# Attention kernel on one core: one product with ones per group of heads, the first pair of key tiles added on VectorE

## The reference

```
h   = layernorm(x) * (scale + 1) + shift
q,k,v = split(h @ w_qkv)                      # 16 heads of 32 channels
q,k = rope(layernorm(q, q_norm_w)), rope(layernorm(k, k_norm_w))
attn = softmax(q @ k^T / sqrt(32))            # 512 x 512 for each head
out = x + (attn @ v) @ w_out * gate
```

## Time and profile before

| | |
|---|---|
| three timed runs | 1797.75 us median (1791.26 to 1800.73) |
| the profiled execution | 1788.8 us, of which 1787.0 us is the span from the first to the last instruction |
| PE busy | 1679.0 us, 94% of the span |
| DVE, ACT, POOL busy | 1245.0, 1036.3, 644.8 us |
| DMA queue of POOL (q0) | 133.18 MB, 39.0% of 16 engines' span |
| granted TensorE clock | 0.980 of full speed, mean over the span |

### The profile page before, as it was taken

One profiled execution on the slowest core, in us unless ns is written; L12 is line 12 of the kernel. 1 busy time (PEld: TensorE's weight loads), 2 busy tenths in 40 slices (PEclk: granted clock), 3 DMA queues, 4 the chain that ended last, 5 costly groups with the idle time before them and its releaser, 6 DMA issues.

```text
span 1787.0 us, 32167 instructions
## 1 busy us (share of the span) xinstructions
PE 1679.0 (94%) x12334; PEld 985.3 (55%) x12334; DVE 1245.0 (70%) x1603; ACT 1036.3 (58%) x1547; POOL 644.8 (36%) x709
## 2 busy tenths in 40 slices
PE   5968999999999999999999999999999999998777
PEld 2734555555555555555555555555555555555444
DVE  8667667777777767777776777777677777766543
ACT  2436556666666666666666666666666665665552
POOL 2423243334334334433433443343344334334222
PEclk8979999999999999999999999999999999999998
DMA  6015355555546555554555555555555555545454
GB/s 208 25 39 109 77 132 112 117 126 111 123 110 137 113 115 127 113 121 110 135 114 116 128 113 118 113 133 115 113 130 113 118 113 133 116 95 118 104 110 124
DMA packets 55566, 205.38 MB, mean 115 GB/s; under 512 B 6888, under 2 KB 6888, under 8 KB 39160
## 3 DMA queue, kind: packets, MB, share of 16 engines
q0 software_dynamic: 18288, 133.18, 39.0%
q1 hardware_dynamic: 37128, 70.14, 11.6%
HBM read 53.25 MB, written 16.88 MB: 39 GB/s over the span
## 4 chain that ended last, share of the span: by engine, by line
PE 85%; ACT 7%; DVE 4%; issue 2%; DMA 1%; SPq 0%; DVEq 0%; ACTq 0%; POOLq 0%
PE SA L412 13%; PE Y L326 11%; PE Y L339 10%; PE Y L329 9%; PE Y L333 9%; PE MB L440 7%; ACT probs L746 7%; PE SM L382 7%; PE O L431 7%; PE MB L361 3%; PE SA L416 3%; DVE cst L987 2%; PE SA L316 1%; PE SA L390 1%; DMA probs<-in_L_cond_w_qkv_dram 1%
## 5 line engine op out<-in xcount | busy, mean ns | idle before, releaser
L987 DVE TENSOR_REDUCE cst<-SM 128x2 fp32r<-128x1024 f32 x256 | 313.4, 1224 | 342.8 <-PE MB L382 342.8
L1208 POOL DMA_DIRECT2D probs<-probs x127 | 109.8, 865 | 812.6 <-ACT probs L748 794.0
L746 ACT ACTIVATE probs<-SM 128x1024 f32<-128x1024 f32 x256 | 262.2, 1024 | 234.8 <-PE SM L416 227.4
L987 DVE TENSOR_REDUCE cst<-MB 128x2 fp32r<-128x1024 f32 x256 | 311.1, 1215 | 0.0
L431 PE MATMUL O<-probs,vals 128*32 128x512 f32 x2048 | 273.8, 607 | 0.0
L748 ACT ACTIVATE probs<-SA 128x1024 f32<-128x1024 f32 x256 | 260.9, 1019 | 0.0
L646 ACT ACTIVATE rows<-Y 128x512 f32<-128x512 f32 x121 | 72.4, 598 | 267.1 <-PE Y L333 267.1
L326 PE MATMUL Y<-wqkv_hi,hT_hi 128*128 128x512 f32 x716 | 216.0, 424 | 0.0
L382 PEld LDWEIGHTS SM<-qk_hi 32*128 32x128 f32 x512 | 51.3, 183 | 258.9 <-issue 78.6
L329 PE MATMUL Y<-wqkv_hi,hT_lo 128*128 128x512 f32 x716 | 193.2, 391 | 0.4 <-DVE hT_lo L969 0.4
L333 PE MATMUL Y<-wqkv_lo,hT_hi 128*128 128x512 f32 x716 | 191.6, 389 | 0.0
(11 more groups left out here) (199 smaller groups left out, 3473.9 us busy)
## 6 DMA issues: line engine op xcount, KB each, us to landing
probs<-probs POOLq DMA_DIRECT2D x127, 1024.0 KB, 7.7
xin<-in_x_dram SPq DMA_DIRECT2D x62, 256.0 KB, 6.8
xres<-in_x_dram SPq DMA_DIRECT2D x60, 256.0 KB, 2.6
out_dram<-xres SPq DMA_DIRECT2D x60, 256.0 KB, 3.7
shift_scale<-mod_rows SPq DMA_DIRECT2D x15, 512.0 KB, 6.0
gate<-mod_rows SPq DMA_DIRECT2D x16, 256.0 KB, 5.2
rows<-in_L_cond_mod_w_dram SPq DMA_DIRECT2D x2, 1024.0 KB, 8.8
probs<-in_L_cond_w_qkv_dram SPq DMA_DIRECT2D x2, 1024.0 KB, 13.2
```

The costliest lines, as they stand in the source:

```text
L746: act.activation(probs[:, a, 2:4, :], SM[:], ACT.Exp).then_inc(s_exp, 1)
L987: dve.tensor_reduce(heads[:, 2 * half:2 * half + 2, 0], bank[:], AX.X, ALU.max, negate=True).then_inc(max_out, 1)
L1208: pool.dma_start(probs[:, probs_buffer(t - 1)].rearrange("p h n -> p (h n)"), probs[:, probs_buffer(t)].rearrange("p h n -> p (h n)"), acc ...
```

## The change

Five things change together, in every stage.

1. The pair is added on DVE. A new function `add_pair(s)` waits for `first_added` and for `weigh_values(s, 2)`, and adds buffer 0 to buffer 2 in one instruction over 128 x 2048 elements. It stands on DVE behind the fourth `maxima` of the stage. The second accumulating transfer, `add_keys(s, 3)`, now waits for this addition (`pair_added`) in place of `weigh_values`. So buffer 2 ends with the sum of all four key tiles.
2. There is one product with ones per group in place of two: `add_over_keys(s - 1)` stands behind `project_out` and before `scores_by_key(s, 2)` of the next stage. The products behind `scores_by_key(s, 1)` and `scores_by_key(s, 3)` are gone.
3. `move_first_sum` on ACT and `add_sums` on DVE are gone. `log_sums` reads PSUM directly and stands, with `inverse_sums`, later on ACT, behind `x_high` and `guess_roots`. `scores_by_query(g, 2)` waits for `sum_ln`; the waits of `scores_by_query(g, 1)` and `(g, 3)` for the sums are gone. The exponentials of tile 0 wait for `pair_added`.
4. On DVE `square_sums(s + 5, 0)` moves from before `low_qk` to behind `maxima(s + 1, 0)`, and `normalize_x` moves from behind the fourth `maxima` to before it.
5. On POOL `add_residual` moves behind the two rotations. At the end of the kernel two products with ones take the place of three, and `add_pair` of the last group stands before `last_parts` on DVE.

```diff
--- before.py
+++ after.py
@@ -131,7 +132,6 @@
             sem("h_hi"), sem("squared"), sem("raw_out"), sem("v_out"), sem("o_out"), sem("qk_high"))
         cT_out, s_exp, sum_ln, sum_ready = sem("cT_out"), sem("s_exp"), sem("sum_ln"), sem("sum_ready")
-        first_summed = sem("first_summed")
         root_ln, root_guess = sem("root_ln"), sem("root_guess")
@@ -142,7 +142,7 @@
         x_scaled, h_lo, qk_low, max_out, o_scaled, y_gated = (
             sem("x_scaled"), sem("h_lo"), sem("qk_low"), sem("max_out"), sem("o_scaled"), sem("y_gated"))
-        sum_added, pass_set = sem("sum_added"), sem("pass_set")
+        pair_added, pass_set = sem("pair_added"), sem("pass_set")
         o_high, o_low, last_high, last_low, wout_low = (
@@ -368,10 +368,8 @@
                     if g == 0:
                         pe.wait_ge(mod_out, 4)
-                if t == 1 and g >= 2:
-                    pe.wait_ge(sum_added, g - 1)
-                if t == 3 and g >= 1:
-                    pe.wait_ge(first_summed, g)
+                if t == 2 and g >= 2:
+                    pe.wait_ge(sum_ln, g - 1)
                 if n > 0:
@@ -433,18 +431,18 @@
                 mm.then_inc(pv_step, 1)
 
-            def add_over_keys(g, t, bank):
-
-                pe.wait_ge(first_added if t == 0 else second_added, 16 * (g + 1))
+            def add_over_keys(g, bank):
+
+                pe.wait_ge(second_added, 16 * (g + 1))
                 for i in range(HG):
-                    mm = pe.matmul(bank[head_rows(i), :], ones_r[:, 0:E].bitcast(F32), probs[:, t, i, :],
+                    mm = pe.matmul(bank[head_rows(i), :], ones_r[:, 0:E].bitcast(F32), probs[:, 2, i, :],
                                    start=True, stop=True, skip_group_check=True)
...
                 for i in range(HG):
                     mm = pe.matmul(MB[head_rows(i), 0, :], ones_r[:, 0:E].bitcast(F32), probs[:, a, i, :],
-                                   start=(a == 0), stop=(a == 1), skip_group_check=True)
+                                   start=(a == 2), stop=(a == 1), skip_group_check=True)
                 if a == 1:
@@ -534,10 +532,6 @@
 
                 scores_by_key(s, 1)
-                if s > 0:
-                    if group(s + 1):
-                        pe.wait_ge(max_out, 2 * TT * (s + 1) + 2)
-                    add_over_keys(s - 1, 2, MB[:, 0, :])
                 weigh_values(s, 0)
@@ -555,6 +549,10 @@
                 if n >= 0:
                     project_out(n, Y[:], 4, 12)
+                if s > 0:
+                    if group(s + 1):
+                        pe.wait_ge(max_out, 2 * TT * (s + 1) + 4)
+                    add_over_keys(s - 1, MB[:, 0, :])
 
@@ -568,9 +566,6 @@
 
                 scores_by_key(s, 3)
-                if group(s + 1):
-                    pe.wait_ge(max_out, 2 * TT * (s + 1) + 6)
-                    add_over_keys(s, 0, MB[:, 0, :])
                 weigh_values(s, 2)
@@ -581,10 +576,9 @@
             project_out(NT - 5, Y[:], 0, 12)
 
-            pe.wait_ge(first_added, 16 * NS)
-            pe.wait_ge(sum_added, LAST)
-            for a in (0, 2):
-                add_last_sums(a)
+            pe.wait_ge(pair_added, NS)
+            pe.wait_ge(sum_ln, LAST)
+            add_last_sums(2)
             pe.wait_ge(last_low, 3)
@@ -700,21 +694,13 @@
                 act.activation(o_hi[:], oT[:, b % 2, :, cols], ACT.Copy).then_inc(o_high, 1)
 
-            def move_first_sum(g):
-                act.wait_ge(ones_done, 2 * g + 1)
+            def log_sums(g):
+                act.wait_ge(ones_done, g + 1)
                 if g > 0:
...
                 else:
                     act.wait_ge(parts_out, 3)
-                act.activation(sum_inv[:], MB[:, 0, :], ACT.Copy).then_inc(first_summed, 1)
-
-            def log_sums(g, sums):
-                if g < LAST:
-                    act.wait_ge(sum_added, g + 1)
-                else:
-                    act.wait_ge(ones_done, 2 * g + 1)
-                    act.wait_ge(o_scaled, g)
-                act.activation(sum_inv[:], sums, ACT.Ln).then_inc(sum_ln, 1)
+                act.activation(sum_inv[:], MB[:, 0, :], ACT.Ln).then_inc(sum_ln, 1)
 
@@ -726,7 +712,7 @@
                     if t == 0:
                         if g > 0:
-                            act.wait_ge(ones_done, 2 * g - 1)
+                            act.wait_ge(pair_added, g)
                         else:
@@ -735,7 +721,7 @@
                     elif t == 2:
                         if g > 0:
-                            act.wait_ge(ones_done, 2 * g)
+                            act.wait_ge(ones_done, g)
                         else:
@@ -822,14 +808,14 @@
                 key_exponentials(s, 1, 0)
                 key_exponentials(s, 1, 1)
-                if s > 0:
-                    log_sums(s - 1, sum_inv[:])
-                    inverse_sums(s - 1)
                 if tile(s + 6):
...
                     guess_roots(s + 7)
 
+                if s > 0:
+                    log_sums(s - 1)
+                    inverse_sums(s - 1)
                 key_exponentials(s, 2, 0)
@@ -841,12 +827,10 @@
                     move_qk(s + 6, 0, Y[:])
                 key_exponentials(s, 3, 0)
-                if s < LAST:
-                    move_first_sum(s)
                 key_exponentials(s, 3, 1)
                 if tile(s + 6):
                     square(s + 6, 0)
-            log_sums(LAST, MB[:, 0, :])
+            log_sums(LAST)
             inverse_sums(LAST)
@@ -987,10 +971,10 @@
                                       ).then_inc(max_out, 1)
 
-            def add_sums(g, bank):
-                dve.wait_ge(ones_done, 2 * g + 2)
-                dve.wait_ge(first_summed, g + 1)
-                dve.tensor_tensor(sum_inv[:], sum_inv[:], bank, ALU.add).then_inc(sum_added, 1)
+            def add_pair(g):
+                dve.wait_ge(first_added, 16 * (g + 1))
+                dve.wait_ge(pv_step, TT * g + 3)
+                dve.tensor_tensor(probs[:, 2], probs[:, 2], probs[:, 0], ALU.add).then_inc(pair_added, 1)
 
@@ -1108,20 +1092,18 @@
 
             for s in range(LAST + 1):
-                if tile(s + 5):
-                    square_sums(s + 5, 0)
                 if group(s + 1):
...
                     low_qk(s + 1, 1)
                     maxima(s + 1, 0)
+                if tile(s + 5):
+                    square_sums(s + 5, 0)
                 if tile(s + 7):
...
                 if tile(s + 5):
                     square_sums(s + 5, 1)
-                if s > 0:
-                    add_sums(s - 1, MB[:, 0, :])
                 if group(s + 1):
@@ -1139,10 +1121,11 @@
                                       ).then_inc(wout_low, 1)
 
+                if tile(s + 7):
+                    normalize_x(s + 7)
                 if group(s + 1):
                     maxima(s + 1, 3)
-                if tile(s + 7):
-                    normalize_x(s + 7)
+                add_pair(s)
                 if s == LAST:
@@ -1204,7 +1187,10 @@
             def add_keys(g, t):
                 pool.wait_ge(s_exp, 2 * (TT * g + t) + 2)
-                pool.wait_ge(pv_step, TT * g + t)
+                if t == 1:
+                    pool.wait_ge(pv_step, TT * g + t)
+                else:
+                    pool.wait_ge(pair_added, g + 1)
                 pool.dma_start(probs[:, probs_buffer(t - 1)].rearrange("p h n -> p (h n)"),
@@ -1231,11 +1217,11 @@
                 if s > 0:
                     scale_o(s - 1)
-                if s - 5 >= 0:
-                    add_residual(s - 5)
                 if tile(s + 5):
                     rotate(s + 5, 0)
                     rotate(s + 5, 1)
+                if s - 5 >= 0:
+                    add_residual(s - 5)
                 if s - 4 >= 0:
```

## The result

The changed kernel takes 1901.83 us in the median of four runs (1898.56 to 1905.5), and the runs of the kernel before have 1799.24 us in the median of four: a ratio of 1.0599 on record, with a 95% interval of 1.0578 to 1.0619. It is 6% slower. (One of the runs of before, at 2069 us, is disturbed and not part of the ratio; the median of the other three is 1797.75 us, and 1901.83 over that is 1.058.) The profiled execution took 1900.72 us, of which the span is 1898.9.

The account below looks back on a forecast made before the run. PE, 94% busy with 85% of the chain, was taken as the bound. Per stage +0.83 + 1.09 - 0.57 = +1.35 us, times 63 = +85; clock +15, end +3 gave 1892, with part of the runs' 9 us 1895 (1808 to 1935).

Parts of the forecast that it names:

- The chain ahead of the exponential: Joint behind key tile 1: fourth maxima, addition, second transfer, then tile 1's exponential at X + 5.60 + L; loses 0.83 us a stage.
- X: Start on PE of `scores_by_query` of the fourth tile, from which the prediction counts times within a stage.
- L = 7.5: Assumed time in us from issue to landing of the second accumulating transfer; ends 6.9 and 9.
- over 1 us each: Sign: ScalarE's first exponential of tile 1 idles this long for the accumulating transfer, in nearly all of 63 cases.
- The product at its new place: Product with ones behind `project_out`, where nothing waits today: costs 1.09 us a stage, ends 0.8 and 1.3.
- The product behind tile 3: Removing the product with ones from the joint behind key tile 3 gains 0.57 us a stage.
- What was hidden: Costed at nothing: `low_qk` fits with 0.1 us; moved square sums hidden by the landing, 0.4 us if it were early.
- The clock: PE's longer idle stretch before the second `scores_by_query` lowers its clock in one stage of seven: 9 x 1.7 = +15 us.
- The end: Kernel's end: last group's `add_pair` waits for `weigh_values` and precedes `last_parts`, so PE's last projection starts later: +3 us once.
- Rival 1: Joint behind tile 1: landing is in time, square sums decide; +0.36 us a stage, 1815 us; chance 0.12.
- Rival 2: PE's busy time counts, joints shrink in full, landing in time: -0.8 us a stage, 1740 us; chance 0.09.
- Rival 3: Landing later still (L = 8.4, +0.9 us a stage) or clock drops in most stages: about 1950 us; chance 0.07.

## Why the prediction was right

It said 1895 us (1808 to 1935), with the landing of the second transfer as the main term; measured were 1901.83. By its steps:

- **The chain ahead of the exponential** (X + 5.60 + L, then 1.17). This was the mechanism, and it held. The addition started at X + 2.83 and took 2.28, the transfer's instruction came at 919.06 = X + 5.66 (predicted 5.55). With a landing of 7.0 the second product is at X + 13.90 where the formula gives 13.77, so its fixed part is 0.13 too short. The halved transfer and the halved addition both moved it the way the chain says.
- **L = 7.5.** Second landings averaged 7.34, from 6.95 to 9.12, but few were near the mean: the median was 6.97, and 13 of 63 took more than 8. A typical stage loses 0.46 us here, not 0.83, and the long landings bring the mean to 0.90. Over 63 stages the piece grew by 54.4 us; predicted were 0.83 x 63 = 52. That the two agree so well is in part luck, since L was too long by 0.16 and the fixed part too short by 0.13. For the same reason the sign "over 1 us each" was met by 22 of the 61 waits only, and the stage of 27.4 us is found neither in the median (27.03) nor in the mean (27.79). What makes a landing long isn't shown by any run.
- **The product at its new place, 1.09.** Measured 1.03 in the median of the changed kernel, 65 of the 86.2 us. The path was the one named: the chain above runs from the product over the logarithm to the exponential of tile 2, at 933.63, which is 2.30 us after the product's start at 931.33 on PE's timeline (predicted 2.35), and ScalarE, which waited for PE ahead of all 64 exponentials of tile 2 before, does so ahead of 5.
- **The product behind tile 3, -0.57.** Measured -0.56, and -0.56 alone in the kernel before.
- **What was hidden.** `low_qk` with 0.1 us to spare: fourth to next first product stayed at 7.06. The square sums: no difference when moved back, and 0.4 us when the landing is early (13.32 measured, against 12.9, which is 13.44 less the 0.57 of the joint). Both as said.
- **The clock, +15.** The rest of the middle piece, 86.2 - 65 = 21 us; 9 of the stages 6 to 58 have more than 8 us there, seven of them 8.8 to 8.9, 1.6 more than the median. The cost of one fall (1.7) was read from a row and held. How often it falls (9) was taken without one, and that it came out is luck: in the middle of the run it fell behind landings of 8.1 us and more (not behind each of them), and the prediction had no count of those.
- **The end, +3.** This term was mis-sized: +6.2. (Its own sum, 1763.2 + 2.3 + 5.2, is 1770.7 and not 1770.8.) The step had `add_pair` of the last group wait for `weigh_values`; it waited for the first transfer, issued at 1863.31 and landed 8.9 us later:

```profile
1872.20 2.29 DVE L977 TENSOR_TENSOR probs<-probs 128x2048 f32<-128x2048 f32 x1 [8.82 <-DMA probs<-probs]
```

PE's last projection started 29.4 us behind X where it was 25.3, and took 4.21 us for nine instructions in place of 2.30, at a granted clock of 0.50 from 1877.74 to 1881.95.

Rival 1 was the kernel without a late landing, at 1815: the halved transfer gave 1813.63 and the kernel without the addition 1811.12, so the condition was the right one and the landing the fact that decided. Rival 2 (PE's busy time is what counts) fell with the product that was worth 0.56 of its 1.07 us. Rival 3's clock lowered in most stages did not come, nor did its landings of 8.4 us as the usual ones.

The rule that spoke for rival 1, in the Trainium skill, "DMA: Bandwidth & Descriptors", section "Anatomy of one DMA — SWDGE (gpsimd) path", can be held against two sizes now. In the median the landings took 6.97 us for 1 MB and 4.55 us for half: 2.4 us for 524288 bytes. If a line may be drawn through two sizes, that is about 217 GB/s, and about 2.1 us that don't depend on size. The trace agrees with the rule's fixed 2.0 us, and not with its 436 GB/s.

## What to carry to other kernels

Before work is put between two transfers, count the chain from what releases the work to who waits for the second transfer, with the shortest landing that the trace has; here 6.1 us were free, 6.9 was the minimum, and a product removed from an engine at 94% turned into 6% more time. A removed instruction is worth what its place lets through: 0.56 us of 1.07 in a joint where PE waits anyway, while the same product costs 1.03 to 1.12 where nothing waited. And when work moves to VectorE, look at what GpSimd runs beside it.

## What the runs showed of the hardware that was not expected

A VectorE instruction with two SBUF inputs and a GpSimd instruction on SBUF don't run side by side here: 0.74 us became 2.67 on GpSimd beside a 2.28 us addition, and 0.74 became 1.73 or 2.61 on VectorE (medians) beside one or two GpSimd instructions that take 1.28 us by themselves. The Trainium skill, "SBUF — State Buffer", section "SBUF: two separate sides", has this as an exclusive lock on a shared pair of ports, held for the whole instruction, whichever engine comes first; the runs agree, with both engines in turn as the one that waits. One wait on GpSimd that keeps them apart was worth 3.5% (1.0169 against 0.9826).
